# Plain float32 for two second-layer groups; normalising on GpSimd and ScalarE instead of VectorE

## The reference

```
x = x + 0.5 * ffn(layernorm(x))
x = x + mixer(layernorm(x))
x = x + 0.5 * ffn(layernorm(x))

ffn(v):  h = layernorm(v) * gamma + beta            # 256 wide
         y = silu(h @ w1 + b1)                      # 1024 wide
         return v + 0.5 * (y @ w2 + b2)             # 256 wide
         # w1, w2: (integer - 128) * scale, one scale per block of 128 rows and column
mixer(v): a = sigmoid(v@Wa+ba); b = v@Wb+bb; c = tanh(v@Wc+bc); d = v@Wd+bd
          s = a*s + (1-a)*b   along the 1024 rows of a sequence
          return (c*s) @ Wy + by + d
```

## Time and profile before

| | |
|---|---|
| median of 3 runs | 855.42 us (855.03 to 856.79) |
| the profiled execution's own time | 857.29 us |
| its span (first to last instruction) | 855.5 us |
| granted TensorE clock, mean | 0.993 |
| PE busy | 814.8 us (95%) |
| DVE busy | 809.2 us (95%) |
| ACT busy | 659.2 us (77%) |
| POOL busy | 559.0 us (65%) |

### The profile page before, as it was taken

How to read it: one execution, slowest core, us unless ns; L and a number is a source line. 1 busy time by engine, 2 the same in 40 slices (tenths; PEclk the granted TensorE clock), 3 DMA queues, 4 the chain that set the end, 5 groups by cost and what they waited for, 6 DMA issues and landing times.

```text
span 855.5 us, 15167 instructions
## 1 busy us (share of the span) xinstructions
PE 814.8 (95%) x3682; PEld 626.2 (73%) x3682; DVE 809.2 (95%) x1645; ACT 659.2 (77%) x1083; POOL 559.0 (65%) x430
## 2 busy tenths in 40 slices
PE   2799999999999999989999999999999999999997
PEld 1477777777777778757777767677777777777785
DVE  5999999999999999889999997999999999999975
ACT  4688888888888888656556567788888888888883
POOL 4676776677677676636556656666766767667763
PEclk9999999999999999999999999999999999999999
DMA  8700000000000000000000000000000110000001
GB/s 262 247 34 2 2 0 0 0 0 0 0 0 0 0 0 1 2 0 2 0 0 0 0 1 0 1 26 25 25 25 26 37 34 25 25 25 25 25 26 51
DMA packets 20619, 20.33 MB, mean 24 GB/s; under 512 B 1590, under 2 KB 20332, under 8 KB 20588
## 3 DMA queue, kind: packets, MB, share of 16 engines
q1 hardware_dynamic: 19180, 17.86, 6.5%
q10 hardware_dynamic: 1312, 2.10, 0.7%
q0 software_dynamic: 96, 0.00, 0.0%
HBM read 11.57 MB, written 8.39 MB: 23 GB/s over the span
## 4 chain that ended last, share of the span: by engine, by line
PE 82%; DVE 10%; issue 3%; ACT 2%; DMA 1%; POOL 1%; DVEq 0%; ACTq 0%; POOLq 0%
PE ps_z L815 40%; PE ps_fc L815 27%; PE ps_fc L905 6%; PE ps_tr L808 3%; PE ps_tr L857 3%; DVE xhat L564 2%; DVE y_sb L596 2%; PE ps_fc L913 1%; DVE z_acc L618 1%; PE ps_fc L899 1%; DVE resid L581 1%; DMA resid<-in_L_attn_x 1%; DVE stats L537 1%; DVE resid L719 1%; PE ps_z L808 1%
## 5 line engine op out<-in xcount | busy, mean ns | idle before, releaser
L349 POOL TENSOR_TENSOR g_lo<-g_full,g_hi 128x512 fp32r<-128x512 f32 x256 | 335.4, 1310 | 186.8 <-ACT g_hi L463 178.9
L447 ACT ACTIVATE u_sb<-ps_fc,cols 128x512 f32<-128x512 f32 x256 | 199.3, 779 | 65.0 <-PE ps_fc L815 62.1
L815 PE MATMUL ps_fc<-h_hi,q_sb 128*128 128x512 f32 x512 | 219.2, 428 | 7.3 <-POOL h_lo L342 3.2
L815 PE MATMUL ps_fc<-h_lo,q_sb 128*128 128x512 f32 x512 | 205.0, 400 | 0.0
L618 DVE SCALAR_TENSOR_TENSOR z_acc<-ps_z,cols,z_acc 128x512 f32<-128x512 f32 x256 | 189.2, 741 | 11.1 <-PE ps_z L815 10.8
L596 DVE SCALAR_TENSOR_TENSOR y_sb<-ps_fc,cols,u_sb 128x512 f32<-128x512 f32 x256 | 189.1, 739 | 10.6 <-ACT u_sb L447 10.6
L461 ACT ACTIVATE g_full<-y_sb 128x512 f32<-128x512 f32 x256 | 159.5, 623 | 38.0 <-DVE y_sb L596 38.0
L564 DVE TENSOR_SCALAR xhat<-resid,mean_var,rstd 128x256 f32 (+1 forms) x192 | 165.4, 907 | 0.0
L463 ACT ACTIVATE g_hi<-y_sb 128x512 fp32r<-128x512 f32 x256 | 158.5, 619 | 0.0
L815 PEld LDWEIGHTS ps_fc<-h_hi,q_sb 128*128 128x128 f32 x512 | 97.7, 191 | 42.7 <-DVE y_sb L596 19.6
L815 PE MATMUL ps_z<-g_hi,q_sb 128*128 128x512 f32 x288 | 116.8, 406 | 2.7 <-DVE z_acc L616 2.2
(11 more groups left out here) (97 smaller groups left out, 1168.2 us busy)
## 6 DMA issues: line engine op xcount, KB each, us to landing
resid<-in_L_attn_x SPq DMA_DIRECT2D x16, 512.0 KB, 4.1
out_x<-resid SPq DMA_DIRECT2D x16, 512.0 KB, 2.9
q_int<-in_L_ffn_fc_q ACTq DMA_DIRECT2D x2, 1024.0 KB, 8.5
z_acc<-in_L_ffn_fc_scales SPq DMA_DIRECT2D x1, 256.0 KB, 7.8
wd_sb<-in_L_attn_Wd SPq DMA_DIRECT2D x1, 256.0 KB
z_acc<-in_L_ffn_fc_scales SPq DMA_DIRECT2D x1, 192.0 KB, 8.5
resid<-in_L_attn_Wy SPq DMA_DIRECT2D x2, 64.0 KB
wab_sb<-in_L_attn_Wa SPq DMA_DIRECT2D x1, 64.0 KB
```

Of the source, the lines that this page charges most:

```text
L349: nc.gpsimd.tensor_tensor(g_lo[:, slot % 4, :], g_full[:, slot % 2, :], g_hi[:, slot % 4, :].bitcast(F32), ALU.subtract).then_inc(g_ready, 1)
L447: nc.scalar.activation(u_sb[:, f % 2, :], ps_fc1[:, f % 2, 0, :], ACT.Identity, bias=col(R_B1 + f), scale=col(R_S1 + f)).then_inc(u_ready, 1)
L815: last = nc.tensor.matmul(out, w, v, start=start and i == 0, stop=stop and i == len(pairs) - 1)
```

## The change

- Groups 0 and 1 of the second layer are "native": real weights in plain float32 (`w2_full`), times `g_native` in plain float32, one product for each half and group (`w2_full[:, g, ...]`), both groups summed in PSUM. Groups 2 to 7 are all whole groups now; scaled groups in two parts are gone. ScalarE makes one silu for a native group instead of two, GpSimd no `g_low`, VectorE no addition; ScalarE's `first_sum` starts `z_acc` for both halves.
- VectorE only makes statistics (step 4). GpSimd makes from them the two terms, the negated mean, the root, and the scale and shift (`rsqrt`, step 6: three small instructions, a wait, the power, a wait, two small ones), then xhat = resid * rstd + shift (`normalise`, step 7) and in steps 1 and 2 of the next tile the residual's scaling (`residual`).
- In the mixer ScalarE normalises, between tanh and `cs_hi`.
- GpSimd's program is written out for all 16 tiles (`each_tile`) rather than looped.

The diff, cut to its core:

```diff
-    SCALED = (4, 3)
-    SUMS = tuple(len(whole) + 1 for whole in whole_groups)
+    NATIVE = 2
+    SPLIT = FC - NATIVE
+    SUMS = SPLIT + 1
...
-    STATISTICS_AT = (1, 2)
-    VARIANCE_AT = 2
-    RSQRT_AT = 2
-    NORMALISE_AT = ((4, 5), (6, 7))
-    RESIDUAL_AT = (6, 7)
-    TURN_AT = ((1, 3), (2, 4))
-    LOWER_PART_AT = ((3, 4), (3, 5))
+    RESIDUAL_AT = (1, 2)
+    STATISTICS_AT = 4
+    RSQRT_AT = 6
+    NORMALISE_AT = 7
+    TURN_AT = (1, 3)
+    LOWER_PART_AT = (3, 5)
...
+        def each_tile(tile):
+            for t in range(NT):
+                tile(t, t % 2, min(t, 2), min(NT - 1 - t, 2))
...
# GpSimd
+            def rsqrt(ln, twice):
+                pool.wait_ge(aggr_done, ln + 1)
+                wait(pool, xhat_ready, ln)
...
+                    nc.gpsimd.tensor_scalar(var_terms[:, 0, :], mean_var[:, :, 1], 1.0 + EPS, EPS * EPS,
+                                            ALU.mult, ALU.add)
+                    nc.gpsimd.tensor_scalar(var_terms[:, 1, :], mean_var[:, :, 1], 4.0, 4.0 * EPS,
+                                            ALU.mult, ALU.add)
...
+                nc.gpsimd.tensor_scalar(neg_mean[:, :], mean_var[:, :, 0], -1.0, 0.0, ALU.mult,
+                                        ALU.add).then_inc(terms_ready, 1)
+                pool.wait_ge(terms_ready, ln + 1)
+                nc.gpsimd.tensor_tensor(rstd[:, 0:n, :], var_terms[:, 0:n, :], minus_half[:, 0:n, :],
                                         ALU.pow).then_inc(rstd_ready, 1)
+                pool.wait_ge(rstd_ready, ln + 1)
+                if twice:
+                    nc.gpsimd.tensor_scalar(res_scale[:, :], rstd[:, 1, :], 1.0, 1.0, ALU.mult, ALU.add)
+                means = neg_mean[:, :].rearrange("p (o a) -> p o a", o=1).broadcast_to([P, n, SUB])
+                nc.gpsimd.tensor_tensor(shift[:, 0:n, :], rstd[:, 0:n, :], means, ALU.mult).then_inc(shift_ready, 1)
+            def normalise(ln, t, blocks=range(SUB)):
+                if blocks[0] == 0:
+                    pool.wait_ge(shift_ready, ln + 1)
+                    wait(pool, turned, 2 * ln)
+                for a in blocks:
+                    last = nc.gpsimd.tensor_scalar(xhat[:, a, :], resid[:, t, a, :], rstd[:, 0, a:a + 1],
+                                                   shift[:, 0, a:a + 1], ALU.mult, ALU.add)
...
+            def residual(ln, t, blocks=range(SUB)):
...
+                for a in blocks:
+                    last = nc.gpsimd.tensor_scalar(resid[:, t, a, :], resid[:, t, a, :], res_scale[:, a:a + 1],
+                                                   shift[:, 1, a:a + 1], ALU.mult, ALU.add)
...
+            def g_low(ff, g, par):
+                if native(g):
+                    return
...
# GpSimd, a tile of a feed-forward
                     for f in range(FC):
+                        if f >= 1:
+                            g_low(ff, f - 1, par)
...
+                            if f == RSQRT_AT:
+                                rsqrt(ln + 2, twice)
+                            if f == NORMALISE_AT:
+                                normalise(ln + 2, t2)
+                        if behind >= 1 and f in RESIDUAL_AT:
+                            residual(ln + 1, t + 1, halves[RESIDUAL_AT.index(f)])
...
# ScalarE
+                if native(g):
+                    wait(act, fc2_done, 2 * step - 14)
+                    nc.scalar.activation(g_native[:, g, :], y_sb[:, g % 4, :], ACT.Silu).then_inc(g_hi_ready, 1)
+                    return
...
# ScalarE in the mixer, after tanh
+                normalise(t + (NT + 2), 1 - behind if behind < 2 else t + 2)
...
# VectorE: variance() without the terms; normalise(), residual_terms(), scale_residual() are gone
-                for a in blocks:
-                    last = nc.vector.tensor_scalar(xhat[:, a, :], resid[:, t, a, :], mean_var[:, a, 0:1],
-                                                   rstd[:, at + a:at + a + 1], ALU.subtract, ALU.mult)
...
# TensorE, fc2
+                    if native(g):
+                        last = nc.tensor.matmul(bank_of(g, n, par), w2_full[:, g, at], g_native[:, g, :],
+                                                start=g == 0, stop=g == NATIVE - 1)
+                    else:
+                        last = products(bank_of(g, n, par), [(w[:, g - NATIVE, at], v[:, split_slot(g, par), :])
+                                                             for w in q2_parts for v in (g_hi, g_lo)])
```

More of the change, by code:

```diff
@@ L247, in filled_before @@
         def filled_before(bank, g, n, ff, par):
-            here = [(j, m) for j in range(FC) for m in (FIRST[j], 1 - FIRST[j])]
+            here = [(j, m) for j in range(FC) for m in range(KC)]
             before = here[:here.index((g, n))] if g < FC else here
@@ L361, in cs_low @@
                 pool.wait_ge(cs_hi_ready, t + 1)
-                if type(t) is int and t == NT - 1:
+                if t == NT - 2:
+                    pool.wait_ge(resid_scaled, NT + 1)
+                elif t == NT - 1:
                     pool.wait_ge(h_ready, 2 * NT + 2)
@@ L373, in tile @@
                     for f in range(FC):
[L374 to L381 removed]
+                        if f >= 1:
+                            g_low(ff, f - 1, par)
+                        elif before:
+                            g_low(ff - 1, FC - 1, 1 - par)
@@ L397, in _ @@
+                    normalise(ln0 + 1, 1)
+                    pool.wait_ge(s2_loaded, 16)
+                    pool.wait_ge(w2_int_ready, 1)
+                    nc.gpsimd.tensor_tensor(w2_full[:, :, :], w2_full[:, :, :], s2_wide,
+                                            ALU.mult).then_inc(w2_ready, 1)
+                each_tile(tile)
+                g_low(ff0 + NT - 1, FC - 1, 1)
             feed_forward(0, 0)
@@ L401, in mixer_tile @@
                     cs_low(t - 1, 1 - par)
-                rsqrt(t + (NT + 2), SUB if behind >= 2 else 2 * SUB)
+                twice = behind < 2
+                rsqrt(t + (NT + 2), twice)
                 for c in range(KC):
@@ L407, in mixer_tile @@
                         h_low(2 * NT, NT, 0, c)
-            over_tiles(pool, mixer_tile)
+                if behind == 1:
+                    residual(t + (NT + 2), 0)
+            each_tile(mixer_tile)
             cs_low(NT - 1, 1)
@@ L526, in mixer_tile, with normalise @@
                 nc.scalar.activation(cs_parts[0:N, par, :], cs_full, ACT.Copy).then_inc(cs_hi_ready, 1)
+            def normalise(ln, t):
+                act.wait_ge(shift_ready, ln + 1)
+                act.wait_ge(turned, 2 * ln)
+                for a in range(SUB):
+                    last = nc.scalar.activation(xhat[:, a, :], resid[:, t, a, :], ACT.Identity,
+                                                bias=shift[:, 0, a:a + 1], scale=rstd[:, 0, a:a + 1])
+                last.then_inc(xhat_ready, 1)
             for c in range(KC):
@@ L534, in _, with statistics, variance @@
         def _(dve):
-            def statistics(t, blocks=range(SUB)):
-                for a in blocks:
+            def statistics(t):
+                for a in range(SUB):
                     last = nc.vector.bn_stats(stats[:, a, :], resid[:, t, a, :])
-                if blocks[-1] == SUB - 1:
-                    last.then_inc(stats_done, 1)
-            def variance(ln, twice):
+                last.then_inc(stats_done, 1)
+            def variance(ln):
                 dve.wait_ge(stats_done, ln + 1)
+                wait(dve, terms_ready, ln)
                 nc.vector.memset(wait_holder[:, :], 0.0)
@@ L637, in tile @@
                         here = f >= LAG
[L638 to L639 removed]
+                        group = (ff if here else ff - 1, (f - LAG) % FC, par if here else 1 - par)
                         if before or here:
@@ L774, in mixer_tile @@
                 nc.vector.tensor_tensor(c_sum, ps_c[0:N, :], c_part, ALU.add).then_inc(c_sum_ready, 1)
-                def norm():
-                    normalise(t + (NT + 2), t2, twice)
-                    if twice:
-                        residual(NT + t2, t2, range(2 if t2 else SUB))
-                if behind:
-                    norm()
                 if before:
```

324 lines of the change are left out of this document (125 added, 199 removed).

## The result

The changed kernel takes 891.95 us (median of four runs, 890.77 to 893.39) and the kernel before, run on the same chip, 855.79 us (855.03 to 856.79). The ratio is 1.0423, with a 95% interval of 1.0403 to 1.0442: slower by 36 us. The forecast was 14 us slower, 870, and its range of 826 to 918 holds the result.

What follows compares the result with a forecast made beforehand. PE (TensorE) and a full DVE bound the kernel before; after, PE waits for GpSimd's row. Loops +19, last stretch -2, start -3, mixer 0: +14 on the 855.4 median, 870 us, range 826 to 918.

Steps and rivals of the forecast that it cites:

- The rival in which the engines' sums decide: Feed-forward tile is PE's 17.9 us plus about 0.9 of short waits, 18.8; total 801 us; chance 0.10.
- R + N: GpSimd's root plus four xhat blocks ahead of `turn`; PE stands still for R + N - 1.98 us a tile.
- the tile's 21.3 us: Feed-forward tile: PE's 17.9 us, a 2.4 wait for GpSimd's xhat, and 1.0 for clock falls.
- the terms put at nothing outside the loops: Mixer: four blocks moved to ACT and small instructions on POOL fit in its 9.3 us a tile, costing 0.
- R: GpSimd's root between two `g_low`: power, five small instructions, two waits; 2.6 us, between 2.3 and 3.4.
- N: Four one-input xhat blocks of 128x256 on GpSimd, 0.45 us each; 1.8 us, between 1.6 and 3.1.
- the two-input line: GpSimd's two-input cost: 0.25 us plus 2.1 ns a column, 0.78 for 256 columns; the high bound for a block.
- the 5.85 that I had: From PE's step 6 to xhat without R and N: 3.20 + 1.25 + 1.25 + 0.15 us.
- the point from which the change costs time: A tile over 20.8 us: R + N about 4.9 without clock falls, about 4.1 with the forecast's share.
- its share of falls: Clock falls from 2.4 to 1.2 GHz behind PE's wait in two of three tiles, 1.0 us a tile average.
- the sum of +19 for the loops: 27 feed-forward tile lengths, each going from 20.6 to 21.3 us: +19 us.
- At the start I had -3: Start: the 3.49 us idle and slow clock go, against some 1.5 us of new GpSimd work: -3 us.

Runs made afterwards that it cites:

- The filled wait: Changed kernel with eight unread products added on TensorE ahead of its wait for xhat before `turn`: 873.97 us, 1.0213.
- 879.79: Changed kernel with the two native groups as one float32r pass, leaving out their lower parts: 879.79 us, 1.0264.
- 864.85: Changed kernel with `turn` in steps 2 and 4 instead of 1 and 3, and what follows it one step later: 864.85 us, 1.0099.
- 793.29: Changed kernel with statistics in step 3, root 4, xhat 6, plus both native groups as one float32r pass: 793.29 us, 0.9272.

## Why the forecast had the direction and missed the size

*The mechanism was right.* A wait of TensorE at `turn` for one row on GpSimd was forecast and is there in 27 of 27 lengths. It goes when the row begins earlier (80 us back), grows by what is put into the row, and doesn't see work beside it. The rival in which the engines' sums decide described another order of the same instructions, 794 us against its 801, not this one.

*The step that failed is the size of R + N in the sum, taken as 4.4 us and measured as 5.02, and with it the tile's 21.3 us; beside it, the terms put at nothing outside the loops.* The tile measured 21.83. R was taken as 2.6 and is 2.84. The five small instructions are 0.19 to 0.20 long, inside the bounds of 0.10 and 0.25, but what counts is the distance of starts: the three ahead of the power start 0.27 apart, the two behind it 0.15. N was taken as 1.8, 0.45 a block, and is 2.18. Its lines in the groups by form (count, busy us, mean ns):

```profile
L365 POOL TENSOR_SCALAR xhat<-resid,rstd,shift 128x256 f32<-128x256 f32 x128 | 69.7, 559 | 0.2
...
L598 ACT ACTIVATE xhat<-resid,shift,rstd 128x256 f32 x48 | 24.7, 586 | 0.2 <-POOL shift L357 0.2
```

The select of 128x128 in the earlier trace rows was too kind a neighbour: a block lies between it and the two-input line, 0.54 between 0.40 and 0.78. (The fixed part of that line, 0.25 in the prediction, works out at 0.21 from its rows.) The Trainium skill (GPSIMD Engine Reference, engine selection) has one-input work at roughly line rate, from which I had estimated N at 1.5; the measured 2.18 is farther from that than from my 1.8. The rest of the row is 0.05 over the 5.85 that I had (3.11, 1.38, 1.28 and 0.13), the row in all 0.67 longer than forecast. PE from `turn` to step 6 took 10.30 and not 10.09: the first product behind four transposes has 0.32 to the next start, not 0.23 (126.87, 127.19, 127.42 above), two such places lie there, and `turn` behind the wait takes 0.40, not 0.35. Together a tile without a fall is 21.2, not 20.3: +0.9, over 27 lengths +24 us. One figure beside the sum is off as well: by the prediction's own terms the point from which the change costs time is R + N of 3.9 with its share of falls, not 4.1.

*The clock was over-priced, which hid a part of it.* Each fall costs 1.55 us (22.75 less 21.20), near the 1.6 that I took from the earlier trace rows, but the clock falls behind about two waits of five, not two of three: 0.62 a tile against 1.0, -10 us over 27. The filled wait shows 18 us as its whole effect in the loops. So the sum of +19 for the loops measured +32.3, by a miss of about +24 and one of about -10 us; that the two have opposite signs is luck.

*Between the loops* I had 0, and it is +4.2. Cut at the first product of each mixer tile in both traces, the parts are +0.9 from the last mark of the first feed-forward to the mixer (with a wait of 2.12 before `turn` at 376.14), +3.0 over the mixer's first three tiles, -0.7 over its next twelve, and +1.1 from its last tile to the first mark of the second feed-forward, where PE stands before `turn` again. The three tiles (granted clock third from the right), then the waits in them and ahead of the second loop:

```profile
383.21:412.04 28.83, 25.83 (x100) 17.45 (x101) 18.58 (x40) 19.21 (x35) 13.36 (x14) 0.88 0.00 1
```

```profile
392.99 1.09 PE L797 MATMUL ps_tr<-ident,xhat 128*128 128x128 f32 x4 [1.42 <-issue]
...
558.95 0.63 PE L797 MATMUL ps_tr<-ident,xhat 128*128 128x128 f32 x4 [3.20 <-issue]
```

In the kernel before the same three tiles take 25.88 us at a clock of 1.00. At 392.99 PE waited 1.42 us for the xhat that ScalarE now makes (it ends at 392.89), and the clock fell behind it, to 0.50 from 393 to 397. At the start I had -3 and it is -0.6: the 3.49 of the earlier trace rows became a wait of 2.31 (26.64) and didn't go, and a new one of 3.14 stands before `turn` in tile 1 (49.88).

*What held.* The last tile and the end: -2.4 for -2. The mixer behind its first tiles: TensorE is as full as in the earlier trace rows though four blocks moved to ScalarE, which takes 0.586 for each, not 0.4, in room it had.

```profile
440.00:480.00 40.00, 40.00 (x188) 29.06 (x187) 26.87 (x66) 30.46 (x55) 24.02 (x33) 1.00 0.00 0
```

A plain float32 product: two weight loads 0.43 apart, as in the earlier trace rows, 0.86 in all. The Trainium skill (FP8 and Floating Point Precision, TensorE Precision Notes) says that true float32 takes four passes through the array. Four float32r distances would be 0.93; this trace decides for 0.86, and it shows two instructions, not how many passes they hold.

```profile
143.80 0.19 PEld L834 LDWEIGHTS ps_z<-g_native,w_full 128*128 128x128 f32 x1 [0.24 <-issue]
144.23 0.19 PEld L834 LDWEIGHTS ps_z<-g_native,w_full 128*128 128x128 f32 x1 [0.24 <-issue]
```

The parts of the miss: loops +13.3, between them +4.2, start +2.4, end -0.4, in all +19.5 of the span (33.5 less 14); the other 2.7 us are the profiled executions' distances from their medians.

## What to carry to other kernels

An engine that is 72% busy can set the loop: follow the unbroken row of its instructions between two marks of the main engine (here step 6 and `turn`) and price its start-to-start distances, the smallest instructions too. Work moved to such an engine is free outside that row (64 us of it cost nothing) and costs more than itself inside (16 us cost 29); so when work moves, move the point from which it can start with it, as the same instructions in steps 3, 4 and 6 gave 794 us and not 892. Time taken from the main engine alone, or a wait pushed to a later step, met the next wait three times (879.79, 864.85, 793.29), so before such an edit look for the second-latest operand.

## What the runs showed of the hardware

GpSimd takes 0.54 us from start to start for a one-input block of 128x256 with two per-partition operands, and 0.15 to 0.27 for one of 128x4 whose own time is 0.20. VectorE makes the same 128x256 block in 0.36 us with GpSimd idle and in 1.21 beside its two-input instructions; ScalarE's take 0.586 each. TensorE's clock went from 2.4 to 1.2 GHz behind some idle times of 2.79 us and stayed at 2.4 behind others of the same length (falls in 11 of 27 tiles); with 3.33 us idle it fell in 18 of 27, at 1.55 us each. It fell behind 1.42 us in the mixer too, and eight idle-filling products took the falls out of the loops.
